# Attention step: the third unit of the maxima in front of the weighing instead of behind it

## What is computed

```python
q = (left @ Wq.T).reshape(N, S, H, Dh)      # N 16, S 1024, H 16, Dh 8
k = (left @ Wk.T).reshape(N, S, H, Dh)
v = (left @ Wv.T).reshape(N, S, H, Dh)
energy = jnp.einsum('nqhd,nkhd->nqkh', q, k)
att = jax.nn.softmax(energy / scale, axis=2)
out = jnp.einsum('nqkh,nkhd->nqhd', att, v)
```

## Time and profile before

| | us |
|---|---|
| median of 3 runs | 3396.84 |
| lowest and highest | 3396.53, 3399.18 |
| span of the profiled execution | 3391.6 |
| TensorE busy, share of the span | 3222.9, 95% |
| VectorE busy, share | 2992.7, 88% |
| ScalarE busy, share | 2843.6, 84% |
| GpSimd busy, share | 897.6, 26% |
| reductions of the units (L966), 3744 from ring_ps | 2369.2, 683 ns each |
| exponentials (L719), 2048 | 1970.1, 1024 ns each |
| matmuls of the weighing (L514), 8192 | 1071.4, 595 ns each |
| matmuls of the units (L481), 3744 into ring_ps | 1086.0, 384 ns each |
| matmuls of the scores (L499), 4096 | 1021.3, 383 ns each |

### The profile page before, as it was taken

How to read it: one execution, slowest core, us unless ns; L and a number is a source line. 1 busy time by engine, 2 the same in 40 slices (tenths; PEclk the granted TensorE clock), 3 DMA queues, 4 the chain that set the end, 5 groups by cost and what they waited for, 6 DMA issues and landing times.

```text
span 3391.6 us, 56526 instructions
## 1 busy us (share of the span) xinstructions
PE 3222.9 (95%) x19712; PEld 941.5 (28%) x19712; DVE 2992.7 (88%) x5577; ACT 2843.6 (84%) x3752; POOL 897.6 (26%) x1322
## 2 busy tenths in 40 slices
PE   6989999999999999999999999999999999999987
PEld 2222232322323232232322323232232322323223
DVE  7999989999898998989989898998989989898943
ACT  3868979798897979979798897979979798896975
POOL 5002050321505123050320505123050320504015
PEclk7998999999999999999999999999999999999999
DMA  3111111121111112121121111112121121111001
GB/s 90 26 41 43 32 50 33 44 50 44 50 31 51 43 39 55 33 61 32 44 49 44 50 31 51 42 39 55 33 61 32 45 49 44 38 32 51 8 22 38
DMA packets 97498, 144.75 MB, mean 43 GB/s; under 512 B 49472, under 2 KB 60096, under 8 KB 89408
## 3 DMA queue, kind: packets, MB, share of 16 engines
q1 hardware_dynamic: 93520, 123.83, 13.8%
q0 software_dynamic: 3696, 17.31, 2.8%
HBM read 34.61 MB, written 32.51 MB: 20 GB/s over the span
## 4 chain that ended last, share of the span: by engine, by line
PE 67%; DVE 17%; ACT 8%; issue 3%; SPq 2%; DMA 1%; POOL 1%; DVEq 0%; POOLq 0%; ACTq 0%
PE heads_ps L514 24%; PE ring_ps L481 15%; DVE max_parts L966 12%; PE scoresT_ps L499 11%; PE scoresT_ps L602 7%; ACT p_sb L719 4%; DVE stats L977 3%; PE scoresT_ps L607 2%; ACT headsT L728 1%; PE ring_ps L543 1%; SPq L346 1%; DVE state L1030 1%; ACT state L784 1%; DVE moments L987 1%; PE ring_ps L529 1%
## 5 line engine op out<-in xcount | busy, mean ns | idle before, releaser
L966 DVE TENSOR_REDUCE max_parts<-ring_ps 128x1 f32<-128x512 f32 x3744 | 2369.2, 683 | 225.4 <-PE ring_ps L481 166.3
L719 ACT ACTIVATE p_sb<-scoresT_ps 128x1024 f32<-128x1024 f32 x2048 | 1970.1, 1024 | 81.4 <-PE scoresT_ps L499 57.7
L481 PE MATMUL ring_ps<-k_rows,q_rows 48*128 48x512 bf16 x3744 | 1086.0, 384 | 33.1 <-DVE max_parts L966 23.8
L514 PE MATMUL heads_ps<-p_sb,v_sb 128*9 128x512 f32 x8192 | 1071.4, 595 | 17.9 <-ACT headsT L728 11.9
L499 PE MATMUL scoresT_ps<-q_rows,k_rows 51*128 51x512 bf16 x4096 | 1021.3, 383 | 7.1 <-ACT p_sb L719 4.3
L481 PEld LDWEIGHTS ring_ps<-k_rows,q_rows 48*128 48x128 bf16 x3744 | 265.5, 94 | 1353.4 <-DVE max_parts L966 1242.4
L1233 POOL CAST max_wide<-max_all 128x16 bf16<-128x16 f32 x128 | 25.4, 198 | 1743.0 <-DVE max_all L972 1743.0
L602 PE MATMUL scoresT_ps<-state,w 128*128 128x512 f32 x732 | 364.9, 621 | 13.3 <-DVE state L1030 12.3
L824 ACT ACTIVATE p_sb<-scoresT_ps,b 128x512 f32<-128x512 f32 x180 | 123.8, 688 | 194.2 <-PE scoresT_ps L602 193.2
L499 PEld LDWEIGHTS scoresT_ps<-q_rows,k_rows 51*128 51x128 bf16 x4096 | 207.0, 93 | 224.4 <-ACT p_sb L719 211.5
L514 PEld LDWEIGHTS heads_ps<-p_sb,v_sb 128*9 128x9 f32 x8192 | 124.4, 88 | 288.8 <-issue 278.3
(11 more groups left out here) (196 smaller groups left out, 2635.9 us busy)
## 6 DMA issues: line engine op xcount, KB each, us to landing
q_rows<-parts SPq DMA_DIRECT2D x744, 32.0 KB
k_rows<-parts SPq DMA_DIRECT2D x744, 32.0 KB
x_sb<-in_x SPq DMA_DIRECT2D x16, 1024.0 KB, 4.8
x_in<-in_x SPq DMA_DIRECT2D x15, 1024.0 KB, 5.4
out<-x_sb SPq DMA_DIRECT2D x15, 1024.0 KB, 3.9
out<-x_in POOLq DMA_DIRECT2D x15, 1024.0 KB, 7.9
q_rows<-max_rows SPq DMA_DIRECT2D x512, 3.0 KB
feat_h<-headsT SPq DMA_DIRECT2D x512, 16.0 KB
```

The lines of the kernel that those rows point to most:

```text
L481: e.matmul(ring_bank(max_taken, u + 1), q_rows[rows, slot, pair, h * BANK + qb * P:h * BANK + (qb + 1) * P], k_rows[rows, slot, pair, kh * ...
L514: m = e.matmul(heads_ps[32 * j:32 * j + DH + 1, :], v_sb[:, b % 2, kb, 4 * (group % NG) + j, 0:DH + 1], p_sb[:, n % 2, j, :], start=(kb == ...
L719: e.activation(p_sb[:, n % 2, 2 * two:2 * two + 2, :].rearrange("p h n -> p (h n)"), scoresT_ps[:, (2 - 2 * two) * BANK:(4 - 2 * two) * BA ...
L966: e.tensor_reduce(max_parts[:, gi % 2, kh, col:col + 1], bank_of(max_taken, u + 1), AX.X, ALU.max).then_inc(max_taken, 1)
```

## The change

In all batches but the first, the count of units by the second place of a step goes from 3n + 2 to 3n + 3. So a step's third unit is issued behind the second pair of scores and in front of the weighing, and none is left for the place behind the weighing. The two units behind the first pair stay. The whole diff:

```diff
--- before.py
+++ after.py
@@ -227,7 +227,7 @@
                 return 0
             if b == 0:
                 return units_until(LEAD0 + 4 * n + (1, 3, 4)[third])
-            return units_until(b * UNITS + LEAD + min(IN_ATTENTION, 3 * n + (2, 2, 3)[third]))
+            return units_until(b * UNITS + LEAD + min(IN_ATTENTION, 3 * n + (2, 3, 3)[third]))
 
         def units_in_beat(b, j):
             if b == -1:
```

## The result

| | before | after |
|---|---|---|
| median of 21 runs each, us | 3397.82 | 3404.11 |
| lowest and highest | 3393.69, 3404.09 | 3401.41, 3410.92 |
| ratio, 95% interval | | 1.002, 1.0014 to 1.0026 |
| span of the profiled execution, us | 3391.6 | 3405.6 |
| mean granted clock of it | 0.985 | 0.981 |

The forecast was 3388.3, 8.5 us faster. The kernel became 6.3 us slower. The measured time lies inside the stated range, 3374 to 3410, but the kernel moved the other way than forecast. The granted clock is the share of TensorE's full clock, 2.4 GHz, that it got on average. In the rows PE is TensorE, PEld its weight loads, DVE VectorE and ACT ScalarE.

What follows compares the result with a forecast made beforehand. A two-step loop through second exponential, weighing and first exponential was taken to set the pace; 4.7 us from groups plus 3.8 us from VectorE's joins gave 8.5 us less, 3388.3 us, range 3374 to 3410.

Steps and rivals of the forecast that it cites:

- The loop over two steps and its parts: Ordinary attention steps: second exponential, weighing, first exponential of a later step; 3.967 us per two steps, forecast 3.955.
- Weighing to E0: From weighing start to a later step's first exponential: forecast 1.435 us, from 1.61 to 1.66; gain 0.20 per link.
- E1 to weighing: From a step's second exponential to the next step's weighing: forecast 1.39 + 0.21 = 1.60 us, bounds 1.59 and 1.61.
- Rival of the release: First score pair's release gains less than 0.20 because units behind it hold back its signal; slower, 3400 to 3420; chance 0.15.
- the group: Eight attention steps from copy to copy of the heads: forecast 16.10 us against 16.14, 4.7 us over 118 groups.
- weighing to weighing: TensorE's own order between two weighing starts without a wait: 1.95 us, forecast unchanged.
- the 0.03 that one parity lost: Every other step, second score pair's halves start apart; forecast that both start at once, taking back 0.03 us.
- a hand-run of after: Links followed through a group's eight steps, with 1.95 as floor: 16.10 us against 16.14.
- the 0.13 of the join steps: Where VectorE joins its parts, a bank wait of 0.13 us, twice in each of 15 batches; forecast to go, 3.8 us.
- 0.3 to spare for the third unit: In join steps, the third unit was to start later behind the weighing, leaving some 0.3 us before its bank binds.
- the single unit waits for its bank: Ahead of the weighing, the unit and the weighing behind it wait for a bank; slower, 11 us, 3408; chance 0.04.

Runs made afterwards that it cites:

- third_133: Against before, in all batches but the first: one unit behind the first score pair, two together between second pair and weighing; 3406.33 us, ratio 1.0031.

## Why the prediction was wrong, point by point

**Right.** The loop over two steps and its parts. Weighing to E0 came at 1.435, the forecast value to the thousandth, in both parities. E1 to weighing in ordinary steps is 1.61 where 1.60 was forecast, and two steps are 3.96 (3.964 with the third decimal), inside the forecast's bounds of 0 to 0.012 less per step. VectorE's and TensorE's counts, batch 0 and the unit-free steps are unchanged. The statement that the edit moves time from one link to another of the same loop holds.

**Rival of the release: fallen.** Two units behind the first pair don't hold back its signal: 1.435 with them, 1.435 without. The Trainium skill (TensorE: Matmul & The Clock Gate, "The cost: per-tile semaphore tail") puts some 26 ns on each signal of matmuls that end together; here the units start 0.22 behind the pair and are as long, so they end behind it, and no run here puts that term to the test. The time did come out inside the 3400 to 3420 of this rival, by luck: the mechanism is another.

**The step that failed first: the group.** The prediction put a group at 16.10; it is 16.173, and 16.139 before. The way from copy to copy passes three links E1 to weighing, one stretch weighing to weighing, and three links weighing to E0. I took 1.60 for each of the first. Two things were mis-sized:

| on the way through a group | forecast | measured |
|---|---|---|
| E1 to weighing behind the copy | 1.60 | 1.649 |
| E1 to weighing, two ordinary | 2 x 1.60 | 2 x 1.611 |
| weighing to weighing | 1.95 | 1.952 |
| weighing to E0, three | 3 x 1.435 | 3 x 1.436 |

Together 0.076 (0.049 + 0.022 + 0.002 + 0.003), all of the gap between 16.10 and 16.173. The largest piece could have been read ahead of the change. Behind the copy the exponentials follow each other without a wait, and each then ends later against its start than the one before, by 0.025 the first time and about 0.014 after that. ScalarE and TensorE of before at the group end of the earlier trace rows, with three rows that the prediction's sum didn't use:

```profile
744.44 1.05 ACT L719 ACTIVATE p_sb<-scoresT_ps 128x1024 f32<-128x1024 f32 x1
```

```profile
745.55 0.39 PE L499 MATMUL scoresT_ps<-q_rows,k_rows 51*128 51x512 bf16 x2
745.87 0.62 PE L514 MATMUL heads_ps<-p_sb,v_sb 128*9 128x512 f32 x4
```

E1 to weighing is 1.43 there (744.44 to 745.87), not 1.39, and with the unit's 0.22 it is 1.65. The other pieces come from rounding a slot of 0.22 down to 0.21.

**Why the sign turned.** The forecast gain of the unit's new place was the 0.03 that one parity lost to halves starting apart. Against before, the same way through a group has +0.219, +0.185 and +0.185 in the links E1 to weighing and three times -0.184 in the links weighing to E0: +0.037. Two of the links earn the 0.034 back, the first doesn't, since behind the copy both halves started together already (745.55). Worked from the rows of before in this way, the sum would have had the right sign. Instead I compared a hand-run of after with the measured 16.14 of before, and took the errors of the hand-run for a gain. The runs show the 0.035 in two pairs of kernels and in the even and odd batches of one. That it is made up in just this way is read from the profile; the two runs meant to separate it changed something else.

**The second step that failed: VectorE.** The prediction let the 0.13 of the join steps go (3.8 us), with 0.3 to spare for the third unit. In the fifth group they stayed whole: 16.298 against 16.173 for the others. In the first group part of them went: what the later join wins back is 0.26 us of an attention in before and 0.18 in after, so of the 3.8 us about 1 came. TensorE, its loads and VectorE of after in the join step of the fifth group:

```profile
775.51 1.04 PE L514 MATMUL heads_ps<-p_sb,v_sb 128*9 128x512 f32 x8
...
777.33 0.09 PEld L481 LDWEIGHTS ring_ps<-k_rows,q_rows 48*128 48x128 bf16 x1 [0.26 <-DVE max_parts L966]
...
777.65 0.62 PE L514 MATMUL heads_ps<-p_sb,v_sb 128*9 128x512 f32 x4
```

```profile
776.59 0.68 DVE L966 TENSOR_REDUCE max_parts<-ring_ps 128x1 f32<-128x512 f32 x1
```

The bank is free 0.74 behind 776.59, at 777.33, and that is where the unit starts; the weighing follows at 777.65, 2.14 behind the one at 775.51, as in the earlier trace rows. The 0.3 to spare were never there. The forecast put the third unit 0.83 to 0.93 behind the weighing's end, by adding its slot to distances of before; but the weighing itself now starts 0.2 later against the exponentials, and the unit stands only 0.67 to 0.72 behind its end (758.36 to 759.03, 756.35 to 757.07). An ordinary step of after:

```profile
758.19 0.68 DVE L966 TENSOR_REDUCE max_parts<-ring_ps 128x1 f32<-128x512 f32 x1
```

```profile
759.03 0.38 PE L481 MATMUL ring_ps<-k_rows,q_rows 48*128 48x512 bf16 x1
```

The bank is free at 758.93, so the room is 0.09 with the third decimal, in both parities. A join holds the reductions up by 0.21, since VectorE first waits for its own last reduction to end. The two kernels with the later join show both sizes: with 0.09 of hold-up instead of 0.21 the 0.13 is gone. The rival "the single unit waits for its bank" was right as a mechanism, in two join steps of an attention, and it took the place of waits in before that cost as much or more, so by itself it doesn't make the kernel slower.

**The clock** had no place in the prediction, beyond TensorE's full clock in the earlier trace rows. Some 2 us of the 7.2 between the means go with it. Why the granted clock is lower with the change (0.9823 against 0.9836), and lower still with the later join (0.981) or with two units ahead of the weighing (0.9817), isn't settled. About 1.4 us, no more than the scatter between sets of runs, remain unexplained.

## What to carry to other kernels

A move inside a closed loop is worth the difference of two nearly equal numbers. Work that difference out from rows of before on both sides, link by link along the way that ends last, with one ruler; don't hold a hand-run of the new kernel against a measured total of the old one. And read each link where the pattern is broken (group ends, joins), not only in ordinary steps: here the ordinary steps were a draw and the broken ones decided. Before putting an instruction ahead of the one that the loop waits for, look up who recycles its bank and what room is left in the shortest step.

## What the runs showed of the hardware

- In a row of exponentials without a wait, each ends later against its start. In ordinary steps an E0 lasts 1.024 and the E1 behind it 1.017; behind a copy they last 1.04 and 1.06, and in after the next two 1.07 and 1.085. Starts there were 0.903 apart and ends 0.917, and what waits for their ends feels it.
- A bank is free for the next matmul's load 0.74 us after the start of a 128x512 reduction (0.68 long) in every kernel looked at.
- Two matmuls on the two halves cost one slot of 0.22 together ahead of a weighing, the same as one (16.176 in third_133 against 16.173 in after for a group).
- TensorE's clock falls to half, 1.2 GHz, for some 3 us now and then, most often 2 to 3 us behind the start of an attention; each time costs 1.6 us there. Ahead of the fall at 2538.5 in after TensorE was busy 86% of 2535 to 2537 and 93% of 2537 to 2539. Executions differ in where and how often, and the time goes with it: 3394 us at a mean granted clock of 0.985, 3400 at 0.982, for the kernel before.
